# Choosing the order of TensorE's products within a step of scores

## What is computed

```
x = x + ssm(layernorm(x))                        # scan over 1024 tokens
x = x + block0(layernorm(x))                     # layer 0
x = x + causal_attention(layernorm(x))           # layer 1
x = x + block2(layernorm(x))                     # layer 2

# each attention: 4 sequences x 16 heads of 8 channels, 1024 x 1024 scores per head
scores = einsum("bhqd,bhkd->bhqk", q, k) * scale # layer 1 adds 32 rotary channels and a causal mask
attn   = softmax(scores)                         # exp(s - max) / sum
o      = einsum("bhqk,bhkd->bhqd", attn, v)
# each mixture of experts (layers 0 and 2): every token goes to one of 8 experts
out    = prob * (act(x @ w1[e]) @ w2[e])
```

## Time and profile before

| | |
|---|---|
| median of 3 runs | 2766.81 us |
| profiled execution: span from first to last instruction | 2676.7 us |
| median less span (what lies around the instructions) | 90.1 us |
| layer 0's tiles, steps 0 to 511 | 117 to 966 us |
| layer 1's tiles, steps 512 to 959 | 966 to 1747 us |
| layer 2's tiles, steps 960 to 1471 | 1747 to 2573 us |
| mean granted TensorE clock | 0.961 |

### The profile page before, as it was taken

One profiled execution on the slowest core, in us unless ns is written; L12 is line 12 of the kernel. 1 busy time (PEld: TensorE's weight loads), 2 busy tenths in 40 slices (PEclk: granted clock), 3 DMA queues, 4 the chain that ended last, 5 costly groups with the idle time before them and its releaser, 6 DMA issues. The chain is left out here.

```text
span 2676.7 us, 44214 instructions
## 1 busy us (share of the span) xinstructions
PE 2323.5 (87%) x15891; PEld 902.8 (34%) x15970; DVE 1899.1 (71%) x3300; ACT 1773.8 (66%) x3759; POOL 890.3 (33%) x1317
## 2 busy tenths in 40 slices
PE   4789989888988998998999999988989988988954
PEld 3222223222322344454444444322223323422424
DVE  6779987878797567656566666787986687697520
ACT  4288877766766666555656656578877777777741
POOL 5450132363254337327415114032023223214124
PEclk7699999999999999999999999999999999999977
DMA  4241103212313421440332122112113312311314
GB/s 161 94 131 28 36 23 107 55 48 85 94 33 100 140 65 58 119 134 24 121 103 70 47 81 68 42 38 68 27 30 114 91 32 85 111 40 54 115 32 169
DMA packets 137888, 205.50 MB, mean 77 GB/s; under 512 B 21130, under 2 KB 104426, under 8 KB 137494
## 3 DMA queue, kind: packets, MB, share of 16 engines
q1 hardware_dynamic: 119238, 141.52, 18.0%
q0 software_dynamic: 17536, 59.58, 7.3%
q10 hardware_dynamic: 896, 1.56, 0.2%
HBM read 138.52 MB, written 60.54 MB: 74 GB/s over the span
## 5 line engine op out<-in xcount | busy, mean ns | idle before, releaser
L1311 ACT ACTIVATE PB<-bank 128x512 f32<-128x512 f32 (+3 forms) x2944 | 1438.0, 556 | 565.8 <-PE bank L999 294.9
L1499 DVE TENSOR_REDUCE small<-unit 128x1 f32<-128x1024 f32 x1024 | 1210.9, 1219 | 243.0 <-PE unit L1019 233.5
L1019 PE MATMUL unit<-RK 61*128 61x512 bf16 (+4 forms) x2762 | 871.0, 375 | 129.3 <-DVE small L1499 74.4
L1139 PE MATMUL bank<-PB,VP 128*32 128x512 f32 (+3 forms) x5888 | 756.1, 567 | 13.4 <-ACT PB L1311 7.8
L999 PE MATMUL bank<-RK 64*128 64x512 bf16 x2048 | 678.2, 387 | 73.6 <-ACT PB L1311 39.9
L1496 DVE CUSTOM_DVE_ANT_0 unit<-unit,maskb 128x640 f32<-128x640 f32 (+7 forms) x512 | 387.6, 770 | 245.7 <-PE unit L1019 228.9
L1019 PEld LDWEIGHTS unit<-RK 61*128 61x128 bf16 (+1 forms) x2816 | 211.4, 95 | 560.2 <-DVE small L1499 230.2
L999 PEld LDWEIGHTS bank<-RK 64*128 64x128 bf16 x2048 | 154.2, 94 | 506.0 <-ACT PB L1311 324.3
L995 PE MATMUL bank<-RK 128*128 128x256 bf16 (+2 forms) x960 | 275.4, 296 | 1.7 <-issue 0.5
L994 PE MATMUL bank<-RK 128*128 128x256 bf16 (+3 forms) x935 | 264.5, 294 | 12.1 <-ACT PB L1311 4.8
L1765 POOL CAST small<-small 128x8 bf16<-128x8 f32 x128 | 24.8, 194 | 621.1 <-DVE small L1499 572.8
(11 more groups left out here) (197 smaller groups left out, 1961.4 us busy)
## 6 DMA issues: line engine op xcount, KB each, us to landing
RK<-qk_parts SPq DMA_DIRECT2D x128, 192.0 KB
qk_parts<-SC SPq DMA_DIRECT2D x48, 384.0 KB, 2.6
RK<-rqk_parts SPq DMA_DIRECT2D x48, 384.0 KB
qk_parts<-SC SPq DMA_DIRECT2D x48, 256.0 KB, 3.0
RK<-qk_parts SPq DMA_DIRECT2D x128, 96.0 KB
XSB<-x_sorted SPq DMA_DIRECT2D x38, 192.0 KB, 4.7
y_sorted<-XSB SPq DMA_DIRECT2D x38, 192.0 KB, 2.1
qk_parts<-SC SPq DMA_DIRECT2D x48, 128.0 KB, 2.9
```

The lines of the kernel that those rows point to most:

```text
L1019: p = e.matmul(unit[k // 2 - 2][:, c0:c1], slot(L, u, 0, 0, rows)[:, 128 * qt:128 * qt + 128], slot(L, u, 1, 0, rows)[:, c0:c1], start=Tru ...
L1139: p = e.matmul(bank[k][32 * j:32 * j + 32, c0:512], VP[:, 8 * (pr // 8) + kt, 9 * h:9 * h + 32], prob(L, t)[:, c0:512], start=(kt == 0), s ...
L1311: e.activation(prob(L, t)[:, c0:512], bank[k][:, c0:512], ACT.Exp, scale=LAYERS[L].scale).then_inc(bank_free[k], 1)
L1499: e.tensor_reduce(m, unit[k // 2 - 2][:, :], AX.X, ALU.max, negate=True).then_inc(bank_free[k], 1)
```

## The change

The order within a step is chosen by the plan, step by step, from four. `late` is how long after TensorE's planned clock the bank of each of the two tiles comes free, `late_unit` the same for the unit. If the first tile's bank is more than 0.3 us later than the unit's, both halves of the unit go first and then both tiles. If the unit is more than 0.5 us later than the second tile, both tiles go first. Else the two kinds alternate, beginning with the unit or with the tile. What is chosen stands in the step (`order`), and `tensor` writes it out. The booking of a step in the plan follows the chosen order; in layers 0 and 2 the first product of a kind costs 0.22 us in the plan, and each one behind it 0.02 until one of the other kind has come.

```
-        P.do("score", h, L=L, mains=mains, units=us)
-        pe = P.at["PE"]
-        for i in range(2):
-            for t, (k, _) in mains[i:i + 1]:
+        order = in_order(h, mains, us)
+        P.do("score", h, L=L, order=order, mains=mains, units=us)
+        pe, shared = P.at["PE"], None
+        for what, i, (a, (k, _)) in order:
+            if what == "main":
...
-                pe = max(pe, P.free[k]) + (0.22 if not ly.causal else 0.12 + (512 - c0) / 1200)
+                pe = max(pe, P.free[k]) + (main_us(shared) if not ly.causal else 0.12 + (512 - c0) / 1200)
...
-                pe += n / 4800 if LAYERS[Lu].causal else 0.02 if mains else 0.22
+                pe += n / 4800 if LAYERS[Lu].causal else main_us(shared)
...
+            shared = None if shared not in (None, what) else what
+    def main_us(shared):
+        return 0.22 if shared is None else 0.02
+
+    def in_order(h, mains, us):
+        t = P.at["PE"]
+        units = [[("unit", i, v) for v in us] for i in range(2)]
+        tiles = [[("main", i, v)] for i, v in enumerate(mains)] or [[], []]
+        late = [max(0.0, P.free[v[1][0]] - t) for v in mains] or [0.0, 0.0]
+        late_unit = max((P.free[v[1][0]] - t for v in us), default=0.0)
+        if late[0] > late_unit + 0.3:
+            return units[0] + units[1] + tiles[0] + tiles[1]
+        if late_unit > late[1] + 0.5:
+            return tiles[0] + tiles[1] + units[0] + units[1]
+        if late[0] > late_unit or late[1] > late_unit + 0.3:
+            return units[0] + tiles[0] + units[1] + tiles[1]
+        return tiles[0] + units[0] + tiles[1] + units[1]
...
                 elif kind == "score":
-                    for i in range(2):
-                        if s.a[0] % 2 == 0:
...
+                    for what, i, (v, use) in s.more["order"]:
+                        if what == "main":
+                            main(s.more["L"], v, use)
                         else:
...
+                            maximum(v, i, use)
```

More of the change, by code:

```diff
@@ L610, in score @@
             us.append((a, max_bank[a]))
-        P.do("score", h, L=L, mains=mains, units=us)
-        pe = P.at["PE"]
-        for i in range(2):
-            for t, (k, _) in mains[i:i + 1]:
+        order = in_order(h, mains, us)
[3 more added lines that the diff above has]
+            if what == "main":
                 ly = LAYERS[L]
-                kt, hh, qh, c0 = ly.mains[t % ly.n2]
+                kt, hh, qh, c0 = ly.mains[a % ly.n2]
                 if kt == 0:
-                    pe = max(pe, sent[L, 2 * (t // ly.n2) + hh])
-                pe = max(pe, P.free[k]) + (0.22 if not ly.causal else 0.12 + (512 - c0) / 1200)
-                before = tile_group(L, t, NPB)
+                    pe = max(pe, sent[L, 2 * (a // ly.n2) + hh])
+                pe = max(pe, P.free[k]) + (main_us(shared) if not ly.causal else 0.12 + (512 - c0) / 1200)
+                before = tile_group(L, a, NPB)
                 ready = max(pe, av_end[before] if before is not None else 0.0)
-                P.free[k] = tile_end[L, t] = P.spend("ACT", ready, 0.07 + (512 - c0) / 970)
-            for (Lu, u, qt), (k, _) in us:
+                P.free[k] = tile_end[L, a] = P.spend("ACT", ready, 0.07 + (512 - c0) / 970)
+            else:
+                Lu, u, qt = a
                 n = 128 * (qt + 1) if LAYERS[Lu].causal else 1024
                 pe = max(pe, P.free[k]) if i == 0 else pe
-                pe += n / 4800 if LAYERS[Lu].causal else 0.02 if mains else 0.22
+                pe += n / 4800 if LAYERS[Lu].causal else main_us(shared)
                 if i == 1:
@@ L1108, in tensor @@
                 elif kind == "score":
-                    for i in range(2):
-                        if s.a[0] % 2 == 0:
[L1111 to L1114, removed]
-                        else:
[L1116 to L1119, removed]
+                    for what, i, (v, use) in s.more["order"]:
+                        if what == "main":
+                            main(s.more["L"], v, use)
+                        else:
+                            maximum(v, i, use)
                 elif kind == "send":
```

## The result

The changed kernel takes 2797.03 us (median of 4 runs, 2790 to 2801) against 2764.82 for the kernel before on the same chip (4 runs): 1.0113 times, 95% interval 1.0090 to 1.0135. Forecast were 2802, 1.3% slower.

What follows compares the result with a forecast made beforehand. Bound: the loop over ScalarE without side work, TensorE's own work beside experts. 14 + 18 + 18 - 15 + 0 = 35 us on 2767 gave 2802 us, 1.3% slower; own range 2777 to 2832, wider range 2752 to 2845.

Steps and rivals of the forecast that it cites:

- 14 + 18 + 18 - 15: Layers 0 and 2: extra slots in steady stretches, beside experts and in the rest, less gain from less TensorE idling, in us.
- The loop over ScalarE and its three banks: Layers 0 and 2 without side work: first tile behind a values' product to ScalarE and back, 2.45 us a loop.
- The steady term: Steady stretches: 67 unit-first steps right behind a values' product start the first tile 0.21 us late, 14 us.
- U U T T costs three slots, 0.21 more than two: Layers 0 and 2: with two unit products before two tile products, only the middle two run together, 0.21 us more.
- Beside experts and in the rest: Layers 0 and 2: 167 steps beside experts pay 18 us; 331 others (projections, norms, batch handover) pay 18, ends 0 and 70.
- The 15 us of gain: Layers 0 and 2: units no longer wait behind tiles lacking a bank; two fifths of 39 us TensorE idling saved.
- Layer 1: a term mis-sized: Layer 1: tiles moved behind late units cost 5 us, tiles put ahead gain as much; 0, 10 us either side.
- Side work: Side work moves by a few steps where the planned clock runs otherwise: a few microseconds of either sign.
- The 90.1 us: Whole kernel: difference between the profile's span of 2676.7 us and the median time, taken as unchanged.
- The terms named for the range: Half to all extra slots beside experts and 0 to 36 us in the rest, given as 2777 to 2832 us.
- the signs: Steady loops 2.66 us, first tile with unit's second half; layer 0 15-25 us longer, layer 2 10-25; less idling before tiles.

Runs made afterwards that it cites:

- alternating: Changed kernel, but in layers 0 and 2 steps with both units or both tiles first are written unit, tile, unit, tile; 2745.55 us, 0.9940; again 2749.56 us, 0.9947.
- old orders: Changed kernel's plan (work, banks, side work), but within each step the old order by even and odd steps; 2776.68 us, 1.0060; again 2780.98 us, 1.0067.
- the steps elsewhere: Changed kernel, but in layers 0 and 2 units first only in the 337 steps not right behind a values' product, the others alternating; 2716.67 us, 1.0147.
- the tiles-first kernel: Changed kernel, but in layers 0 and 2 tiles first in the 228 steps right behind a values' product, all others alternating; 2707.47 us, 1.0107.
- the second profile of the kernel before: Kernel before run and profiled again, nothing edited; 2763.56 us, 1.0014.

## Why the prediction was right, and where it was not

The sum of 35 us and the measured 32 agree by luck, because errors met. On the chips where the kernel before takes 2764 us, as differences of the ratios times that:

| part | forecast | measured |
|---|---|---|
| unit or tile pairs in layers 0 and 2 | 14 + 18 + 18 - 15 = 35 | +48 and +46 (changed less alternating) |
| the other new orders, nearly all in layer 1 | 0 | -33 and -33 (alternating less old orders) |
| moved side work and banks | a few | +17 and +19 (old orders less before) |
| sum | 35 | 31 and 32 |

From the medians instead of the ratios the three parts are 49 and 43, -31 and -31, 14 and 16: each is known to within 10 us.

**What bounds the kernel: right.** The loop over ScalarE and its three banks sets the steady stretches; every edit that left the first tile's signal alone left the loop at 2.45 or 2.46, and those that delayed it gave 2.70.

**The steady term: the right number by the wrong step.** Steps 64 to 127 went from 81.2 us to 85.9, and steps 1024 to 1087 from 80.9 to 85.6: 0.15 a loop on average. Over all steady stretches that makes some 16 us, an estimate, where 14 were forecast. The step that failed is "U U T T costs three slots, 0.21 more than two". The rows from which I took it (like products 0.21 apart) are sound, but they do not say that a product of the other half of the rows waits for its turn in the program. It doesn't: it starts ahead. Its completion does wait. (The words on the kernel before have TensorE execute its list strictly in order. For the ends of these products that holds, for their starts it doesn't.) The Trainium skill ("TensorE: Matmul & The Clock Gate", section "Part 3: Packing small matmuls — row/col tiling") has matmuls in program order at both start and end; by that U U T T would have cost the slots I summed. The trace disagrees on the starts and agrees on the ends. On the first tile behind an `av` a lost slot and a late signal look the same; the steps elsewhere and the tiles-first kernel tell them apart.

**Beside experts and in the rest:** 36 us less 15 gained were forecast from slots that are not lost. Some 30 us are paid there on top of the steady 16. The late signal can act there too, whenever ScalarE has no other tile, but which of those steps pay was not separated. From the first tile of step 1152 to that of step 1216, beside experts, the new plan takes 120.4 and 120.6 us with old orders, 120.5 and 119.7 alternating, and 125.7 and 123.2 in the changed kernel (two profiles of each). The 15 us of gain don't show. They were to come from less idling of TensorE before tiles whose bank ScalarE still holds. That idling grew, from 50.8 us in the second profile of the kernel before to 76.3 in the changed kernel. What shrank is the idling before units for VectorE's reductions in layers 0 and 2, from 72.1 to 29.7:

```profile
L1019 PE MATMUL unit<-RK 61*128 61x512 bf16 (+4 forms) x2816 | 904.4, 380 | 129.1 <-DVE small L1499 72.1
L999 PE MATMUL bank<-RK 64*128 64x512 bf16 x2048 | 689.7, 393 | 93.5 <-ACT PB L1311 50.8
```

```profile
L1040 PE MATMUL unit<-RK 61*128 61x512 bf16 (+4 forms) x2764 | 816.1, 378 | 69.6 <-DVE small L1514 29.7
L1020 PE MATMUL bank<-RK 64*128 64x512 bf16 x2048 | 682.3, 392 | 125.7 <-ACT PB L1326 76.3
```

**Layer 1: a term mis-sized.** I put 0 with 10 either side, weighing tiles moved behind late units against tiles moved ahead of them as equals. The plan sees most late units coming: on the old plan the waits fell from 48 to 8 and the layer got 9 to 18 us shorter, on the new plan from 47 to 25 or 26, and 28 us shorter.

**Side work: taken as a few microseconds, it costs 17 to 19.** On the new plan with old orders layer 1 takes 823 us. Its waits have one that the old plan has not, of the projection for GpSimd's scaling:

```profile
PE bank L1187 <- POOL W L1773: 10.1, 1, 10.1
```

But the alternating kernel has it too, and takes 794 us there:

```profile
PE bank L1190 <- POOL W L1776: 9.4, 1, 9.4
```

So this wait alone doesn't make the 823. The late units are 34 us with old orders and 21 with the new ones. Why the old orders are so poor a match for the new places, and the new ones a good one, was not taken apart.

**The 90.1 us:** "taken as unchanged" did no harm, as the sum was a difference. But the profile on which I read the expert stretches was of a chip without the holds.

**The range and the signs.** The terms named for the range give 14 + 18 + 0 - 15 = 17 to 14 + 35 + 36 - 15 = 70, so 2784 to 2837, and not 2777 to 2832. Of the signs, the layers' lengths came as forecast, though of other parts. The loop was 2.70 and not 2.66, the first tile started with the first half of the unit and not the second, and idling before tiles grew.

## What to carry to other kernels

Where matmuls of two row halves share the array, order them by whose completion somebody waits for, not only by whose operands are ready: a product may run beside an earlier one and still be told done behind it. A rule that is right in one stage (tiles ahead of a late unit, in the causal layer) can be paid for by another stage where its second branch sits on the loop; try it stage by stage: with the old plan, the rule in layer 1 alone gives 0.9938. And profile on the chip on which you time, or at least see that span and time agree.

## What the runs showed of the hardware

- TensorE started a matmul of the other row half ahead of an earlier one that waited for its half: 310 steps with the program U U T T and starts U, T at 0, U, T at 0.22. Its semaphore came 34 ns after the earlier one's: 0.644 us from start to semaphore, not 0.401, and 0.73 from start to ScalarE's start, not 0.48.
- Two kinds of chip. On one, all of TensorE is held 14 to 19 times in an execution, for 0.7 to 8.8 us each, 59 to 73 us in sum, about where GpSimd issues the experts' and the collecting indirect transfers; on the other never. The same kernel takes 2763 and 2677 us. In the layers' tiles the granted clock is at the lower level for 149 us on the one and 72 on the other. What holds TensorE stays open. Each group of runs had one chip, so a difference between hours would look the same as one between chips.
- The holds do not simply add. Layer by layer the old plan takes 849, 781 and 826 us without them, and 875, 793 and 854 with them. The new plan takes 848, 789 and 841 without (tiles first behind an `av`) and 876, 793 and 846 with (alternating); both take 81 us for steps 64 to 127. So in layers 1 and 2 the new plan is 8 and 15 us behind the old one where there are no holds, and level and 8 us ahead where there are. The changed kernel itself was not run without them.
